# A four-layer graph network: how the running maxima of a window's 16 chunk ends are chained on VectorE

## The chip, the cores and the metric

The kernel runs on one core of one Trainium2 chip. The metric is the device time of one execution in microseconds (us), as the median of several executions. PE is TensorE, DVE is VectorE, ACT is ScalarE, POOL is GpSimd and SP is SyncE, which here only starts DMAs.

## The reference

Four graph layers run one after the other on 3125 nodes of 256 features and 50,000 edges; each is followed by a residual sum and a layer norm. Layers 1 and 2 are attention layers. For each edge a score per head is computed (4 heads in layer 1, 8 in layer 2), and then a softmax over all edges that end in the same node:

```python
m = jax.ops.segment_max(score, col_idx, num_segments=n)
ex = jnp.exp(score - m[col_idx])
denom = jax.ops.segment_sum(ex, col_idx, num_segments=n)
alpha = ex / denom[col_idx]
agg = jax.ops.segment_sum(alpha[..., None] * msg_edge, col_idx, num_segments=n)
```

The edges are sorted by their target node, so a node's edges are a run of neighbours in the order (a segment). The first two layers' inputs are gathered rows of tables, 128 edges at a time.

## The kernel before

**Chunks and windows.** The sorted edges are laid out in NCH = 416 chunks of 128 edges, one edge per partition. WIN = 16 chunks make a window, so each attention layer ("pass") has NW = 26 windows. `Attend` holds what both passes share, `Attend1` (4 heads, names a1, rows of 516 values) and `Attend2` (8 heads, a2, rows of 520 values) what differs. POOL gathers one row per edge into a ring of 36 slots by an indirect DMA per chunk (L2132), and it may refill a slot when PE has summed the chunk that lay in it.

**The work on a chunk.** In pass 1, PE fetches the queries of the chunk's targets with a one-hot matmul (L2480, three products for each chunk), DVE multiplies them with the gathered keys for two chunks at a time (L2494) and reduces four chunks' products at a time to scores (L2501). In pass 2 a score is only a sum of two gathered numbers (L2593, L2597). When the scores of a whole window are there, the window's chain gives the exponentials. Then ACT multiplies the values with them (L2531 in pass 1, L2624 in pass 2, where DVE does every other part, L2613), PE sums the chunk by target with a one-hot matrix (`total`, L2535 or L2629), and DVE adds the sum to the accumulator of the node tile (`add`, L2538 or L2635). `total(n)` waits until the sum of chunk n - 3 (pass 1) or n - 2 (pass 2) has been added, because its PSUM banks are used in turn. `add(n)` waits until `add(n - 1)` has ended. Before `add(n)` with n a multiple of 8, DVE's sequencer loads eight tile numbers into registers (`slots`).

**The loop.** Each engine runs a loop over w (the window whose chain is made) and i = 0..15. In step i of window w the engine also works on chunk n = 16 (w - 1) + i of the window before, and on scores of the window behind. So chain, sums and scores are woven together in the fixed order of each engine's own program. The tables `CHAIN`, `TURNS`, `SCORES` and `FETCHES` say at which i a part stands; for DVE an entry (i, False) stands ahead of `add(n - 2)` and (i, True) behind it.

**The chain of a window.** (1) PE turns the scores so that a row is one chunk and one head with its 128 edges in a line ("score", i = 5 in pass 1). (2) `run` and `most` are a forward and a backward scan over the 128 edges, with state = max(state + mask, value); a mask entry is 0 inside a segment and -1e30 where one ends. `most` is then the maximum of each segment within its chunk. (3) A segment can go on over several chunks. So the first and the last entry of each row are picked (`ends_in`) and a matmul (`ends`) brings them to one row per head: 16 values of the first edges and 16 of the last edges. Ten small DVE operations on [heads, 16] tiles then carry the maximum over the chunks, with the row vectors `seams` (0 where a chunk goes on with the segment that the chunk before it ended in), `whole` (0 where a chunk is one segment) and `through` (their sum): `carry` (scan), `onto`, `lead`, `past`, `tail`, two copies of one element, `last_in` (backward scan), `through`, `first`. They are at (8, False), (8, True), (9, False) and (9, True). (4) A matmul (`spread`, i = 10) brings the results `first_last` back to the rows; `picked`, `edge`, `most_1` and `most_2` put them into the row maxima. (5) PE turns `most_2` back ("back", L2383, i = 12 in pass 1 and 13 in pass 2), DVE makes `fall` (L2281, how much the maximum of the open node rose) and `below` (score minus maximum), and ACT makes the exponentials behind `keep_r` (L2335, i = 14).

**Order between engines** is by semaphores alone. Every step of the chain adds one to the semaphore `chain`; `after(name)` makes the sequencer wait until that step has ended:

```python
if at == here["lead"]:
    after("onto")
    step("lead", e.tensor_tensor(self.lead[:, :], self.onto[:, :], small[0:H, 0:WIN], ALU.max))
    after("lead")
    step("past", e.tensor_tensor(self.past[:, 0:WIN - 1], self.lead[:, 1:WIN], seams[:, 1:WIN], ALU.add))
```

`Segments.vector_ends` makes `seams`, `whole` and `through` once, in the stage ahead of pass 1.

Of the kernel before, what the change touches and what calls it, by code (L numbers as in the profile page):

```python
# [15 lines left out]
BF16 = mybir.dt.bfloat16  # L16
U16 = mybir.dt.uint16
ALU = mybir.AluOpType
# [1926 lines left out]
class Segments:  # L1945
# [3 lines left out]
    def __init__(self, b, ctx, slot_rows):  # L1949
        sb = lambda n, s, d=F32: b.sb(n, s, d, ctx)  # L1950
        self.seams, self.whole, self.through = (sb(n, [H2, NCH], BF16) for n in ("seams", "whole", "through"))
# [61 lines left out]
    def vector_ends(self, e):  # L2013

        kept, finish = self.kept, self.finish
        e.wait_ge(self.back, 16 * 3)
        e.memset(self.seams[:, 0:1], 0.0)
        e.tensor_tensor(self.seams[:, 1:NCH], self.first[:, 1:NCH], self.last[:, 0:NCH - 1], ALU.is_equal)
        e.tensor_tensor(self.whole[:, :], self.first[:, :], self.last[:, :], ALU.is_equal)
        e.tensor_copy(self.opens[:, :], self.local_f[:, 0:NCH:WIN]).then_inc(kept, 1)  # L2020
        e.wait_ge(kept, 4)
        finish(e, self.seams[:, :], self.seams[:, :])
        finish(e, self.whole[:, :], self.whole[:, :]).then_inc(kept, 1)
        e.wait_ge(kept, 5)
        e.tensor_tensor(self.through[:, :], self.seams[:, :], self.whole[:, :], ALU.add).then_inc(kept, 1)
        e.wait_ge(kept, 6)
# [16 lines left out]
class Attend:  # L2043


    def __init__(self, b, seg, own, name, heads, acc, table, word, stride, parts, x, lent=0):
# [10 lines left out]
        if x is not None:  # L2057
# [10 lines left out]
        self.ends_in, self.picked, self.edge = sb("ends_in", [R, 2, WIN]), sb("picked", [R, 2, WIN]), sb("edge", [R, 2])  # L2068
        self.carry = sb("carry", [H, 2, WIN + 1])
        self.onto, self.lead, self.past, self.tail = (sb(n, [H, WIN]) for n in ("onto", "lead", "past", "tail"))  # L2070
        self.last_in, self.first_last = sb("last_in", [H, WIN]), sb("first_last", [H, 2, WIN])
# [14 lines left out]
    STEPS = ("run", "most", "ends_in", "open", "carry", "onto", "lead", "past", "tail", "last_in", "through", "first",  # L2086
             "picked", "edge", "most_1", "most_2", "fall", "below")
# [73 lines left out]
    def constants_vector(self, e):  # L2161
# [4 lines left out]
        e.memset(self.carry[:, 0, 0:1], -BIG)  # L2166
# [25 lines left out]
    def vector(self, e):  # L2192
# [23 lines left out]
        def chain(w, i, late):  # L2216
# [7 lines left out]
            c = self.carry[:, w % 2, :]  # L2224
            both = self.first_last
            seams, whole, through = (t[0:H, w * WIN:(w + 1) * WIN] for t in (seg.seams, seg.whole, seg.through))
# [9 lines left out]
            if at == here["ends_in"]:  # L2236
                after("most")
                step("ends_in", e.tensor_tensor(self.ends_in[:, :, :], self.k1[:, :].unsqueeze(1).to_broadcast([R, 2, WIN]),
                                                self.most[:, 0:P:P - 1].unsqueeze(2).to_broadcast([R, 2, WIN]), ALU.mult))
# [4 lines left out]
            if at == here["carry"]:  # L2244
                e.wait_ge(self.ends_out, self.w0 + w + 1)
                step("carry", e.tensor_tensor_scan(c[:, 1:WIN + 1], through, small[0:H, WIN:2 * WIN], c[:, 0:1], ALU.add, ALU.max))
                after("carry")
                step("onto", e.tensor_tensor(self.onto[:, :], c[:, 0:WIN], seams, ALU.add))
            if at == here["lead"]:
                after("onto")  # L2250
                step("lead", e.tensor_tensor(self.lead[:, :], self.onto[:, :], small[0:H, 0:WIN], ALU.max))
                after("lead")
                step("past", e.tensor_tensor(self.past[:, 0:WIN - 1], self.lead[:, 1:WIN], seams[:, 1:WIN], ALU.add))
            if at == here["tail"]:
                after("past")
                step("tail", e.tensor_tensor(self.tail[:, 0:WIN - 1], self.past[:, 0:WIN - 1], c[:, 1:WIN], ALU.max))
                e.tensor_copy(both[:, 1, WIN - 1:WIN], c[:, WIN:WIN + 1])
                e.tensor_copy(self.carry[:, (w + 1) % 2, 0:1], c[:, WIN:WIN + 1])
                after("tail")
                step("last_in", e.tensor_tensor_scan(both[:, 1, WIN - 2::-1], through[:, :0:-1], self.tail[:, WIN - 2::-1],  # L2260
                                                     c[:, WIN:WIN + 1], ALU.add, ALU.max))
            if at == here["through"]:
                after("last_in")
                step("through", e.tensor_tensor(self.last_in[:, :], both[:, 1, :], whole, ALU.add))
                after("through")
                step("first", e.tensor_tensor(both[:, 0, :], self.last_in[:, :], self.lead[:, :], ALU.max))
            if at == here["picked"]:
                e.wait_ge(self.spread, self.w0 + w + 1)
                step("picked", e.tensor_tensor(self.picked[:, :, :], small[0:R, 64:64 + 2 * WIN].rearrange("r (a k) -> r a k", a=2),
                                               self.k1[:, :].unsqueeze(1).to_broadcast([R, 2, WIN]), ALU.mult))  # L2270
                after("picked")
                step("edge", e.tensor_reduce(self.edge[:, :], self.picked[:, :, :], AX_X, ALU.add))
# [1566 lines left out]
```

## Time and profile before

| | |
|---|---|
| median of 3 executions | 3441.07 us (3435.51 to 3443.51) |
| profiled execution, first to last instruction (span) | 3438.5 us |
| PE busy | 2897.5 us, 84% |
| DVE busy | 2544.3 us, 74% |
| POOL busy | 2183.2 us, 63% |
| ACT busy | 1935.0 us, 56% |
| mean granted PE clock | 0.884 |
| pass 1, `run` of window 0 to `run` of window 25 | 1384.2 to 1953.8 us |
| pass 2, the same | 2156.9 to 2703.0 us |

The page gives no time for the profiled execution besides its span, which lies between the lowest and the highest of the three times and 2.6 us under their median. The two passes take about 1130 us of it, a third. The busy shares are means over six stages that have little in common, so they say nothing of what a change in the passes is worth; the length of one window of a pass does.

### The profile page before, as it was taken

To read this page: it belongs to the slowest core of one execution; us is meant where nothing else is said; L and a number is where in the kernel's file an instruction comes from. 1 tells how busy PE (TensorE), PEld (TensorE's weight loads), DVE (VectorE), ACT (ScalarE), POOL (GpSimd) and SP (SyncE) were. 2 spreads that over 40 slices of the span, in tenths; PEclk is the share of its full clock that TensorE was granted. 3 is DMA by queue.
4 is the path that set the end of the run, shared out by engine and by line. 5 is a ranking of instruction groups with operands and counts; after the bars stand their busy time and mean duration, and the time that the engine had idled before them with its cause. 6 is when DMAs were issued, how large, how long until landed. Compare 5 with 4: busy or idle time off the path is not lost. (4 is left out here: it accounts for less than half of the span.)

```text
span 3438.5 us, 60509 instructions
## 1 busy us (share of the span) xinstructions
PE 2897.5 (84%) x15715; PEld 1839.2 (53%) x15715; DVE 2544.3 (74%) x6536; ACT 1935.0 (56%) x6284; POOL 2183.2 (63%) x2289
## 2 busy tenths in 40 slices
PE   5799889999988896788888866899999897788875
PEld 4666555555555553455555544677777653333332
DVE  8899789999977554888888843799999874444444
ACT  0478655555541452687788722688888753333333
POOL 1777677777756532766666355777777314777774
PEclk9999899999999998798899988899999996655665
DMA  5334388888851789777777555777777444333334
GB/s 179 100 104 130 121 256 261 260 265 264 261 138 34 242 324 351 243 229 220 218 209 212 128 186 184 224 227 227 228 228 226 117 199 162 104 103 103 103 104 103
DMA packets 260604, 651.44 MB, mean 189 GB/s; under 512 B 66781, under 2 KB 115626, under 8 KB 253498
## 3 DMA queue, kind: packets, MB, share of 16 engines
q0 software_dynamic: 141840, 474.50, 45.9%
q1 hardware_dynamic: 118442, 173.08, 15.5%
q8 instruction: 149, 2.44, 0.3%
q14 instruction: 173, 1.42, 0.1%
HBM read 505.42 MB, written 145.27 MB: 189 GB/s over the span
## 5 line engine op out<-in xcount | busy, mean ns | idle before, releaser
L2132 POOL DMA_INDIRECT a_rows<-table,met x568 | 560.3, 987 | 241.1 <-issue 137.8
L3729 PE MATMUL ps<-rows_in,hot_w 128*128 128x256 f32 x832 | 431.5, 630 | 114.2 <-ACT hot_w L3691 68.5
L1330 POOL DMA_INDIRECT rows_in<-table,met x416 | 413.1, 993 | 142.9 <-issue 80.3
L3679 POOL DMA_INDIRECT rows_in<-table,met x416 | 404.2, 972 | 144.3 <-issue 118.3
L3754 DVE TENSOR_TENSOR xs<-xs,ps 128x256 f32 x416 | 175.1, 421 | 302.7 <-PE ps L3729 298.1
L3729 PEld LDWEIGHTS ps<-rows_in,hot_w 128*128 128x128 f32 x832 | 192.6, 284 | 353.1 <-ACT hot_w L3691 199.2
L3691 ACT ACTIVATE hot_w<-hot,met 128x128 f32<-128x128 f32 x416 | 166.7, 402 | 372.1 <-PE ps L3729 353.9
L2629 PE MATMUL ps<-a_rows,a_hot 128*128 128x260 f32 x1136 | 316.4, 402 | 18.2 <-DVE acc L2635 12.7
L2132 POOL DMA_INDIRECT xs<-table,met x264 | 258.7, 980 | 107.3 <-issue 61.3
L833 POOL DMA_INDIRECT records<-rec,rows x241 | 260.5, 1081 | 87.6 <-issue 72.9
L2635 DVE TENSOR_TENSOR acc<-acc,ps 128x520 f32 x416 | 287.0, 690 | 34.6 <-PE ps L2629 13.6
L2624 ACT ACTIVATE a_rows<-a_rows 128x64 f32<-128x64 f32 x1136 | 281.2, 334 | 0.0
L2531 ACT ACTIVATE a_rows<-a_rows 128x64 f32<-128x64 f32 x1104 | 274.2, 335 | 0.0
L1362 ACT ACTIVATE z<-z 128x512 f32<-128x512 f32 x208 | 131.1, 631 | 243.8 <-DVE z L1491 243.8
L1440 PE MATMUL ps<-rows_in,hot_w 128*128 128x272 f32 x832 | 244.5, 417 | 3.7 <-ACT hot_w L1377 3.7
L1403 PE MATMUL ps<-by_dst,hot_t 128*128 x1248 | 212.0, 278 | 35.7 <-issue 32.0
L2629 PEld LDWEIGHTS ps<-a_rows,a_hot 128*128 128x128 f32 x1136 | 194.5, 191 | 68.4 <-issue 32.9
L2480 PE MATMUL ps<-q_parts,a_hot_t 128*128 x1248 | 208.9, 312 | 14.7 <-DVE a_prod L2494 8.2
L2535 PE MATMUL ps<-a_rows,a_hot 128*128 128x260 f32 x568 | 197.5, 441 | 26.2 <-DVE acc L2538 22.2
L1476 DVE TENSOR_TENSOR acc<-acc,ps 128x272 f32 x416 | 180.6, 434 | 47.4 <-DVE acc L1476 42.0
L2538 DVE TENSOR_TENSOR acc<-acc,ps 128x260 f32 x416 | 174.1, 419 | 50.0 <-issue 22.4
L620 ACT ACTIVATE film_room<-film_room,code_parts 128x128 bf16<-128x128 bf16 x648 | 191.7, 387 | 20.2 <-DVE film_room L716 20.2
(492 smaller groups left out, 6417.3 us busy)
## 6 DMA issues: line engine op xcount, KB each, us to landing
a_hot_t<-one_hots SPq DMA_DIRECT2D x104, 256.0 KB, 5.0
table<-stage SPq DMA_DIRECT2D x25, 1024.0 KB, 3.9
rows_in<-table,met POOLq DMA_INDIRECT x832, 3.8
one_hots<-hot_t SPq DMA_DIRECT2D x52, 256.0 KB
dst_row<-slot_rows SPq DMA_DIRECT2D x51, 256.0 KB, 5.0
by_dst<-dst_rows SPq DMA_DIRECT2D x25, 512.0 KB, 5.7
by_dst<-lo_rows SPq DMA_DIRECT2D x24, 512.0 KB, 4.4
a_rows<-table,met POOLq DMA_INDIRECT x568, 3.8
```

The source lines that it names most:

```text
L833: e.indirect_dma_start(b.meta, bass.IndirectOffsetOnAxis(ap=r.rows[:, c:c + 1], axis=0), r.rec[:, c, :], None).then_inc(s, 16)
L1330: e.indirect_dma_start(self.rows[:, n % self.RING, 0:2 * D], None, self.table, bass.IndirectOffsetOnAxis(ap=self.b.met[:, n, R_SRC:R_SRC + ...
L1403: e.matmul(out, self.hot_t[:, half, k, :], row[:, m * D:(m + 1) * D], start=(m == 0), stop=False)
L1440: e.matmul(b.ps[:, 4 + n % 4, 0:D + ET], self.hot_w[:, n % self.AHEAD, :], self.rows[:, n % self.RING, D:2 * D + ET], start=True, stop=Tru ...
L2132: e.indirect_dma_start(self.row(n, 0, self.width), None, self.table, bass.IndirectOffsetOnAxis(ap=b.met[:, n, self.word:self.word + 1], ax ...
L2480: last = e.matmul(out, hot_t, row[:, k * D:(k + 1) * D], start=(k == 0), stop=(k == 2))
L2531: last = e.mul(value, value, row[:, 2 * D + h:2 * D + h + 1])
L2624: last = e.mul(value, value, row[:, h:h + 1])
L2629: last = e.matmul(self.b.ps[:, 2 + 2 * (n % 2) + g, 0:GW2], hot, self.group(n, g), start=True, stop=True)
L2635: return e.tensor_tensor(both, both, self.b.ps[:, at:at + G2, 0:GW2], ALU.add)
L3679: e.indirect_dma_start(self.rows[:, n % self.RING, :], None, self.table, bass.IndirectOffsetOnAxis(ap=self.b.met[:, n, R_REL:R_REL + 1], a ...
L3729: e.matmul(b.ps[:, n % self.BANKS, 0:D], self.hot_w[:, n % GRP_H, :], self.rows[:, n % self.RING, :], start=True, stop=True).then_inc(self ...
```

## The change

The two ends of a chunk are put next to each other: one row of 32 entries per head holds first edge, last edge, first edge, last edge and so on, where there were two rows of 16. One mask row `links` with the same layout (the link into a chunk, then the link through it) takes the place of `seams`, `whole` and `through`; it has one more pair at its end, filled by a memset. A forward scan (`ahead`) over 32 entries and a backward scan (`both`) over the result give what the ten steps gave. The last entry of `ahead` is the carry into the next window, kept in two buffers in turn. `ahead` stands at (8, False) and `both` at (8, True); nothing of the chain is left at i = 9. PE's matmuls `ends`, `spread` and the others stay at their i, and `spread` waits for `both` where it waited for `first`. `ends_in` and `picked` have the same number of elements in another order, `edge` reduces along a stride of two. The core of the diff:

```diff
-        self.seams, self.whole, self.through = (sb(n, [H2, NCH], BF16) for n in ("seams", "whole", "through"))
+        self.links = sb("links", [H2, NCH + 1, 2], BF16)
...
-        e.memset(self.seams[:, 0:1], 0.0)
-        e.tensor_tensor(self.seams[:, 1:NCH], self.first[:, 1:NCH], self.last[:, 0:NCH - 1], ALU.is_equal)
-        e.tensor_tensor(self.whole[:, :], self.first[:, :], self.last[:, :], ALU.is_equal)
+        e.memset(self.links[:, 0, 0:1], 0.0)
+        e.memset(self.links[:, NCH, 0:2], 0.0)
+        e.tensor_tensor(self.links[:, 1:NCH, 0], self.first[:, 1:NCH], self.last[:, 0:NCH - 1], ALU.is_equal)
+        e.tensor_tensor(self.links[:, 0:NCH, 1], self.first[:, :], self.last[:, :], ALU.is_equal)
         e.tensor_copy(self.opens[:, :], self.local_f[:, 0:NCH:WIN]).then_inc(kept, 1)
         e.wait_ge(kept, 4)
-        finish(e, self.seams[:, :], self.seams[:, :])
-        finish(e, self.whole[:, :], self.whole[:, :]).then_inc(kept, 1)
+        finish(e, self.links[:, :, :], self.links[:, :, :]).then_inc(kept, 1)
         e.wait_ge(kept, 5)
-        e.tensor_tensor(self.through[:, :], self.seams[:, :], self.whole[:, :], ALU.add).then_inc(kept, 1)
-        e.wait_ge(kept, 6)
 
...
-        self.ends_in, self.picked, self.edge = sb("ends_in", [R, 2, WIN]), sb("picked", [R, 2, WIN]), sb("edge", [R, 2])
-        self.carry = sb("carry", [H, 2, WIN + 1])
-        self.onto, self.lead, self.past, self.tail = (sb(n, [H, WIN]) for n in ("onto", "lead", "past", "tail"))
-        self.last_in, self.first_last = sb("last_in", [H, WIN]), sb("first_last", [H, 2, WIN])
+        self.ends_in, self.picked, self.edge = sb("ends_in", [R, WIN, 2]), sb("picked", [R, WIN, 2]), sb("edge", [R, 2])
+        self.ahead, self.both = sb("ahead", [H, 2, 2 * WIN]), sb("both", [H, 2 * WIN])
...
-    STEPS = ("run", "most", "ends_in", "open", "carry", "onto", "lead", "past", "tail", "last_in", "through", "first",
-             "picked", "edge", "most_1", "most_2", "fall", "below")
+    STEPS = ("run", "most", "ends_in", "open", "ahead", "both", "picked", "edge", "most_1", "most_2", "fall", "below")
...
-        e.memset(self.carry[:, 0, 0:1], -BIG)
+        e.memset(self.ahead[:, 1, 2 * WIN - 1:2 * WIN], -BIG)
...
-            c = self.carry[:, w % 2, :]
-            both = self.first_last
-            seams, whole, through = (t[0:H, w * WIN:(w + 1) * WIN] for t in (seg.seams, seg.whole, seg.through))
+            ahead, before = self.ahead[:, w % 2, :], self.ahead[:, (w + 1) % 2, 2 * WIN - 1:2 * WIN]
+            links = seg.links[0:H, :, :].rearrange("h k a -> h (k a)")
+            at_0 = 2 * w * WIN
...
-                step("ends_in", e.tensor_tensor(self.ends_in[:, :, :], self.k1[:, :].unsqueeze(1).to_broadcast([R, 2, WIN]),
-                                                self.most[:, 0:P:P - 1].unsqueeze(2).to_broadcast([R, 2, WIN]), ALU.mult))
+                step("ends_in", e.tensor_tensor(self.ends_in[:, :, :], self.k1[:, :].unsqueeze(2).to_broadcast([R, WIN, 2]),
+                                                self.most[:, 0:P:P - 1].unsqueeze(1).to_broadcast([R, WIN, 2]), ALU.mult))
                 if w:
                     e.wait_ge(self.scale_out, self.w0 + w)
                 step("open", e.tensor_scalar(self.open_hot[:, :], b.iota[0:H, :], d0, None, ALU.is_equal))
-            if at == here["carry"]:
+            if at == here["ahead"]:
                 e.wait_ge(self.ends_out, self.w0 + w + 1)
-                step("carry", e.tensor_tensor_scan(c[:, 1:WIN + 1], through, small[0:H, WIN:2 * WIN], c[:, 0:1], ALU.add, ALU.max))
-                after("carry")
-                step("onto", e.tensor_tensor(self.onto[:, :], c[:, 0:WIN], seams, ALU.add))
-            if at == here["lead"]:
-                after("onto")
-                step("lead", e.tensor_tensor(self.lead[:, :], self.onto[:, :], small[0:H, 0:WIN], ALU.max))
-                after("lead")
-                step("past", e.tensor_tensor(self.past[:, 0:WIN - 1], self.lead[:, 1:WIN], seams[:, 1:WIN], ALU.add))
-            if at == here["tail"]:
-                after("past")
-                step("tail", e.tensor_tensor(self.tail[:, 0:WIN - 1], self.past[:, 0:WIN - 1], c[:, 1:WIN], ALU.max))
-                e.tensor_copy(both[:, 1, WIN - 1:WIN], c[:, WIN:WIN + 1])
-                e.tensor_copy(self.carry[:, (w + 1) % 2, 0:1], c[:, WIN:WIN + 1])
-                after("tail")
-                step("last_in", e.tensor_tensor_scan(both[:, 1, WIN - 2::-1], through[:, :0:-1], self.tail[:, WIN - 2::-1],
-                                                     c[:, WIN:WIN + 1], ALU.add, ALU.max))
-            if at == here["through"]:
-                after("last_in")
-                step("through", e.tensor_tensor(self.last_in[:, :], both[:, 1, :], whole, ALU.add))
-                after("through")
-                step("first", e.tensor_tensor(both[:, 0, :], self.last_in[:, :], self.lead[:, :], ALU.max))
+                step("ahead", e.tensor_tensor_scan(ahead, links[:, at_0:at_0 + 2 * WIN], small[0:H, 0:2 * WIN], before, ALU.add, ALU.max))
+            if at == here["both"]:
+                after("ahead")
+                step("both", e.tensor_tensor_scan(self.both[:, ::-1], links[:, at_0 + 1:at_0 + 2 * WIN + 1][:, ::-1], ahead[:, ::-1],
+                                                  -BIG, ALU.add, ALU.max))
             if at == here["picked"]:
                 e.wait_ge(self.spread, self.w0 + w + 1)
-                step("picked", e.tensor_tensor(self.picked[:, :, :], small[0:R, 64:64 + 2 * WIN].rearrange("r (a k) -> r a k", a=2),
-                                               self.k1[:, :].unsqueeze(1).to_broadcast([R, 2, WIN]), ALU.mult))
+                step("picked", e.tensor_tensor(self.picked[:, :, :], small[0:R, 64:64 + 2 * WIN].rearrange("r (k a) -> r k a", a=2),
+                                               self.k1[:, :].unsqueeze(2).to_broadcast([R, WIN, 2]), ALU.mult))
                 after("picked")
-                step("edge", e.tensor_reduce(self.edge[:, :], self.picked[:, :, :], AX_X, ALU.add))
+                step("edge", e.tensor_reduce(self.edge[:, :], self.picked[:, :, :].rearrange("r k a -> r a k"), AX_X, ALU.add))
...
-                step("fall", e.tensor_scalar(self.fall[:, :], both[:, 0, 0:1], c[:, 0:1], 0.0, ALU.subtract, ALU.max))
+                step("fall", e.tensor_scalar(self.fall[:, :], self.both[:, 0:1], before, 0.0, ALU.subtract, ALU.max))
...
-            flat = lambda t: t[:, :, :].rearrange("r a k -> r (a k)")
-                e.matmul(small[0:H, 0:2 * WIN], self.of_head[:, :], flat(self.ends_in), start=True, stop=True).then_inc(self.ends_out, 1)
+                e.matmul(small[0:H, 0:2 * WIN], self.of_head[:, :], self.ends_in[:, :, :].rearrange("r k a -> r (k a)"), start=True, stop=True).then_inc(self.ends_out, 1)
-                e.wait_ge(self.chain, self.chained(w, "first"))
-                e.matmul(small[0:R, 64:64 + 2 * WIN], self.to_rows[:, :], flat(self.first_last), start=True, stop=True).then_inc(self.spread, 1)
+                e.wait_ge(self.chain, self.chained(w, "both"))
+                e.matmul(small[0:R, 64:64 + 2 * WIN], self.to_rows[:, :], self.both[:, :], start=True, stop=True).then_inc(self.spread, 1)
...
-    CHAIN = {"run": (5, True), "most": (6, False), "ends_in": (6, True), "carry": (8, False), "lead": (8, True), "tail": (9, False),
-             "through": (9, True), "picked": (10, True), "most_1": (11, False), "fall": (11, True), "below": (12, False)}
+    CHAIN = {"run": (5, True), "most": (6, False), "ends_in": (6, True), "ahead": (8, False), "both": (8, True), "picked": (10, True), "most_1": (11, False), "fall": (11, True), "below": (12, False)}
```

The same `CHAIN` edit stands in `Attend2`. STEPS has 12 names for 18, so `chain` counts to other values. The wait behind `vector_ends` in the stage ahead of pass 1 is for `kept` 5 where it was 6. Nothing else of the kernel is touched.

## Rows read from the trace of the kernel before

**Rows 1.** Busy time of each engine in the steady part of pass 1 and of pass 2 (us; PE, PEld, DVE, ACT, POOL, each with its instructions, then granted PE clock, DMA share, GB/s).

```profile
1405.00:1954.00 549.00, 457.84 (x2541) 308.15 (x2540) 476.15 (x1202) 442.35 (x1745) 359.80 (x378) 0.89 0.74 215
2199.00:2681.00 482.00, 459.26 (x3042) 343.13 (x3041) 438.67 (x1075) 409.75 (x1604) 359.38 (x354) 1.00 0.78 227
```

**Rows 2.** The scan `run` in each pass: count, ns min/median/max, first and last start.

```profile
L2232 DVE TENSOR_TENSOR_SCAN a_run<-a_mask,ps x25: 403/405/405, 1405.3 to 1953.8; 64x128 f32<-64x128 bf16 x25
L2232 DVE TENSOR_TENSOR_SCAN a_run<-a_mask,ps x23: 409/411/414, 2199.6 to 2680.3; 128x128 f32<-128x128 bf16 x23
```

**Rows 3.** Waits from 1400 to 2040 us: us in total, times, longest.

```profile
ACT a_keep_r L2335 <- DVE a_fall L2281: 63.1, 24, 3.1
...
PE ps L2383 <- DVE a_most L2277: 52.5, 25, 2.4
...
PE ps L2535 <- DVE acc L2538: 31.9, 85, 1.2
```

**Rows 4.** DVE timeline of one window of pass 1: start, us, and in brackets idle before.

```profile
1704.16 0.23 DVE L2246 TENSOR_TENSOR_SCAN a_carry<-through,a_carry,ps 4x16 f32<-4x16 bf16 x1
...
1704.61 0.42 DVE L2538 TENSOR_TENSOR acc<-acc,ps 128x260 f32 x1
...
1705.61 0.23 DVE L2260 TENSOR_TENSOR_SCAN a_first_last<-through,a_carry,a_tail 4x15 f32<-4x15 bf16 x1
1705.78 0.42 DVE L2538 TENSOR_TENSOR acc<-acc,ps 128x260 f32 x1
...
1706.31 0.16 DVE L2266 TENSOR_TENSOR a_first_last<-a_last_in,a_lead 4x16 f32<-4x16 f32 x1
1707.37 0.42 DVE L2538 TENSOR_TENSOR acc<-acc,ps 128x260 f32 x1 [0.90 <-issue]
```

**Rows 5.** PE timeline of the same window, around its wait for the chain.

```profile
1707.94 0.68 PE L2535 MATMUL ps<-a_rows,a_hot 128*128 128x260 f32 x2 [0.48 <-DVE acc L2538]
...
1710.76 0.37 PE L2383 MATMUL ps<-ident,a_most 64*128 64x64 f32 x1 [2.15 <-DVE a_most L2277]
```

**Rows 6.** Groups of DVE instructions by shape, both passes: busy us, mean ns | idle before.

```profile
L2235 DVE TENSOR_TENSOR_SCAN a_most<-a_mask,a_run 64x128 f32<-64x128 bf16 x26 | 10.8, 414 | 0.9
...
L2246 DVE TENSOR_TENSOR_SCAN a_carry<-through,a_carry,ps 4x16 f32<-4x16 bf16 x26 | 5.9, 226 | 0.0
```

**Rows 7.** Columns of rows 1: behind a stall, and two whole windows of pass 1.

```profile
1711.50:1717.50 6.00, 6.00 (x27) 4.15 (x27) 4.91 (x9) 5.74 (x23) 2.80 (x3) 0.53 0.70 225
...
1611.20:1633.30 22.10, 18.47 (x108) 12.53 (x106) 19.64 (x51) 17.97 (x72) 15.50 (x17) 0.92 0.78 229
...
1701.80:1725.20 23.40, 19.82 (x108) 13.26 (x106) 19.97 (x51) 18.35 (x73) 14.38 (x16) 0.85 0.66 197
```

**Rows 8.** DVE timeline, the one wait for PE of over 0.25 us in the window from 1611.2.

```profile
1626.52 0.42 DVE L2538 TENSOR_TENSOR acc<-acc,ps 128x260 f32 x1 [0.67 <-PE ps L2535]
```

**Rows 9.** PE timeline at shorter stalls of another stage.

```profile
407.06 0.21 PE L673 MATMUL ps<-prod,above 25*25 25x1 f32 x2 [0.59 <-DVE prod L772]
407.96 0.96 PE L675 MATMUL ps<-reached,ones 25*128 25x416 f32 x2 [0.70 <-DVE reached L776]
...
1063.29 1.97 PE L1673 MATMUL ps<-up,h_t 128*128 128x256 f32 x8 [1.14 <-DVE y L1749]
```

**Rows 10.** Columns of rows 1: the granted clock at the stalls of rows 9.

```profile
409.00:413.00 4.00, 4.00 (x15) 1.82 (x14) 0.54 (x1) 0.00 (x0) 0.96 (x1) 0.60 0.72 180
1062.00:1066.00 4.00, 2.86 (x15) 2.43 (x14) 3.03 (x8) 0.89 (x3) 3.41 (x5) 1.00 0.21 68
```

**Rows 11.** POOL timeline in pass 1, one of the gathers that follow one another.

```profile
1630.41 0.95 POOL L2132 DMA_INDIRECT a_rows<-table,met  x1 [0.30 <-issue]
```

**Rows 12.** Waits from 2160 to 2720 us (pass 2): us in total, times, longest.

```profile
PE ps L2629 <- DVE acc L2635: 19.1, 90, 0.5
```

**Rows 13.** PE timeline in pass 2 beside the chain's small steps (DVE makes them from 2421.76 to 2424.56).

```profile
2423.31 1.11 PE L2629 MATMUL ps<-a_rows,a_hot 128*128 128x260 f32 x4
...
2424.64 1.12 PE L2629 MATMUL ps<-a_rows,a_hot 128*128 128x260 f32 x4
```

More of the change, by code:

```diff
@@ L2554 @@
     TURNS, HOT_AT, OTHER_AT = {"score": 3, "ends": 7, "spread": 10, "back": 13}, 2, 8
-    CHAIN = {"run": (4, True), "most": (5, True), "ends_in": (6, True), "carry": (8, False), "lead": (8, True), "tail": (9, False),
-             "through": (9, True), "picked": (11, True), "most_1": (12, True), "fall": (13, False), "below": (14, False)}
+    CHAIN = {"run": (4, True), "most": (5, True), "ends_in": (6, True), "ahead": (8, False), "both": (8, True), "picked": (11, True), "most_1": (12, True), "fall": (13, False), "below": (14, False)}
     def __init__(self, b, seg, own, acc, table, parts, x):
@@ L2765, in sync @@
         self.seg.sync(e)
-        e.wait_ge(self.seg.kept, 6)
+        e.wait_ge(self.seg.kept, 5)
         for t in range(NS - self.QS, NS):
```

## The prediction

> **What bounds the kernel now.** I read the page's slices first: the two passes are stages in which PE, DVE, ACT and POOL are all busy, so the table by stage comes next [rows 1]. DVE is busy for 87% of pass 1 and 91% of pass 2, PE for 83% and 95%; the granted clock is 0.89 in pass 1 and 1.00 in pass 2. The unit to reason in is the window. From the first and last `run` scan a window takes (1953.8 - 1405.3) / 24 = 22.85 us in pass 1 and (2680.3 - 2199.6) / 22 = 21.85 us in pass 2 [rows 2].
>
> In pass 1 the waits say who is late [rows 3]: PE waits for `most_2` 25 times, 52.5 us together, and ACT for `fall` 24 times, 63.1 us. That is 2.1 and 2.6 us in each window, and both ends of the wait are the chain on DVE. The DVE timeline shows why: from `carry` to the `add` of chunk 8, at 1704.16 to 1707.37, DVE goes from one small step to the next with no gap of its own but the 0.90 us of `slots` [rows 4]. PE stops 2.15 us for the result [rows 5]. So DVE sets the time from i = 0 to i = 12, and a microsecond taken from it there comes out of the window, as long as PE still waits at "back".
>
> Behind each such stall PE runs at the lower clock: from 1711.5 to 1717.5 the mean granted clock is 0.53, where 0.50 is 1.2 of 2.4 GHz, and PE is busy all six microseconds [rows 7]. There PE sets the time, and DVE waits for it; even in one of the short windows it waits 0.67 us in one piece [rows 8]. The two whole windows show what it costs. At a mean clock of 0.92 the low stretch is 2 x 0.08 x 22.1 = 3.5 us long, at 0.85 it is 2 x 0.15 x 23.4 = 7.0 us, and the windows last 22.1 and 23.4 us: 1.3 / 3.5 = 0.37 us for each us of low clock. At the pass's mean of 0.89 that is 5.0 us of it and 1.9 us of time in each window, an estimate by a straight line.
>
> **The change, part by part.** *What it takes away.* Ten operations between `carry` and the `add` of chunk 8. Start to start this stretch is 1707.37 - 1704.16 = 3.21 us, with two adds (chunks 6 and 7) in it.
>
> *What it puts there.* Two scans of 32 entries. No row has this width. Scans of 128 take 0.414 us and scans of 16 take 0.226 us [rows 6], so 32 lies between them; on the line between them it is 0.226 + 16 x 0.188 / 112 = 0.253 us, which I take, since 32 is nearer to 16. The upper end would add 2 x 0.16 = 0.32 us to each window. Start to start counts, not the record: `last_in` (0.23) is followed by an independent `add` after 0.17 [rows 4], so 0.06 of a record lies under the next. New stretch: `ahead` 0.19, `add` of chunk 6 0.34 (0.42 less some 0.08), `both` 0.19, then `add` of chunk 7 and the `add` of chunk 8 behind its eight register loads. From `first` to that `add` it takes 1.06 now [rows 4], and the loads can start when chunk 7's `add` has been handed over, so again 1.06. Sum 0.19 + 0.34 + 0.19 + 1.06 = 1.78 us, which saves 3.21 - 1.78 = 1.43 us. If the loads hid nothing and both scans cost the upper end, 0.7 us would be left; if the loads hid under `both` too, 1.6.
>
> The waits of `both` on `ahead` cost nothing: the `add` of chunk 6 lies between them. If it did not, it would be some 0.07 us. `spread` stays at i = 10, and `both` is ready well ahead of it.
>
> *Where the stall goes.* The `add` of chunk 8 comes 1.43 earlier too, and PE's sum of chunk 11 waited 0.48 us for it [rows 5]. With that and its short wait for `first` gone PE reaches "back" about 0.7 us earlier and `most_2` comes 1.43 earlier: the stall shrinks from 2.15 to about 1.45 us. It is still there, so DVE is still what sets the time and the whole 1.43 counts: x 25 windows (the first starts behind other waits) = 35.8 us.
>
> *Equal work in another order.* `ends_in`, `picked`, `edge`: the same elements, at strides; `fall`, the masks and the PE matmuls: unchanged in size. `vector_ends` loses one tensor addition, once, before pass 1. All these count as nothing; DVE has no wait on their layout that a row could show, and if each of the three cost 0.05 us more on DVE, it would be 0.15 x 25 = 4 us, which is inside the range.
>
> *The clock.* Does PE keep 2.4 GHz through a stall of 1.45 us? The rows on both sides are near: 1.14 us of waiting kept it at 1.00, while 0.59 and 0.70 us of waiting close together were followed by a mean of 0.60 [rows 9, 10]. So I expect most windows to drop as before and let one in four keep the clock. If a window keeps it, the 1.9 us come back only as far as POOL allows: a gather takes 0.95 + 0.30 = 1.25 us [rows 11], sixteen 20.0, and some 20.2 with the slower ones. From 22.85 - 1.43 = 21.42 that leaves 1.2 us. One in four: 0.3 x 25 = 7.5 us; none 0; all 30.
>
> The Trainium skill, "TensorE: Matmul & The Clock Gate", Part 1, says that the throttled clock is the default and recent activity lifts it. The falls behind stalls in pass 1 agree (clock 0.53 behind a 2.15 us wait); by that rule alone a shorter stall can only help, and the time would tend to the all-windows case below.
>
> The skill's "DVE: opcode table, instruction layouts, handler registers and perf-mode slots", section 6, speaks against wide scans: the built-in scan runs at half throughput. The two scan rows differ by 0.188 us over 112 entries, 1.7 ns an entry. At the clock in "VectorE: DVE Perf Modes" (0.96 GHz), half throughput would be 2.1 ns, an estimate, and the 32 added entries would cost 0.07 us a window instead of 0.05: no matter here.
>
> *Pass 2.* PE is busy 95% [rows 1] and runs its sums back to back beside the chain's small steps: 1.11 us from 2423.31, then other matmuls, then the next sum at 2424.64 with no wait named [rows 13]. Its waits for DVE adds sum to 19.1 us in 90 pieces [rows 12], 0.7 us a window, mostly away from these steps. So the removed work lies under PE. Bounds 0 and 19 us; I take 3.
>
> *Sum.* 35.8 + 7.5 + 3 = 46 us off the span of 3438.5, to 3392; the median of the runs is 2.6 us above that span, so 3394.6, which I give as 3394.
>
> **The rivals.** *A, my forecast:* pass 1 gives the chain's 1.43 us, a minority of windows keeps the clock: 3385 to 3410.
>
> *B, the clock stays up in nearly all windows of pass 1.* For it: the shorter stall, and the 1.14 us that was survived. Against: the pair of 0.59 and 0.70 that was not. Then a window meets POOL's 20.2: (22.85 - 20.2) x 25 = 66, and 3 in pass 2: 3372; with half of the windows 3387.
>
> *C, part of the gain is taken by another engine in pass 1.* POOL is already at its 1.25 us cadence over long runs, and ACT, which waits 2.6 us now, would have 1.2 left. If half of the 1.43 goes, and the clock gives nothing: 18 + 1 off, 3422. For it: ACT, PE and POOL are all above 65% in pass 1. Against: each has over 1.43 us of waiting in a window.
>
> *D, nothing measurable:* the window is set by PE and the chain only fills DVE's wait for it. It would be 3434 to 3448. Against it stand the 52.5 us in which PE waits. That two scans cost what ten steps did is excluded by the 0.414 us row.
>
> *E, slower: the lower clock spreads.* Windows end at another point against the clock's changes, and the low stretch behind the stall could get longer. It decides when it grows by more than 1.43 / 0.37 = 3.9 us, from 5.0 to 8.9 us. If it grew to 12 us in each window: 7 x 0.37 - 1.43 = 1.16 us, x 25 = 29 slower, 3470. Against: 7.0 us is the longest in the rows of whole windows.
>
> **How the numbers follow.** A 0.60, B 0.17, C 0.16, D 0.04, E 0.03. No more than about 0.2% of the time (7 us) can be told from no change here. Faster is A, B and C: 0.93; same is D: 0.04; slower is E: 0.03. The predicted time is A's 3394. The range leaves out D, E, the upper part of C and nothing of B: 3372 to 3420.
>
> **What the profile after would show.** `ahead` and `both` at 0.24 to 0.27 us each. 8 x 52 = 416 fewer DVE instructions in the passes. Carry-to-chunk-8 stretch 1.8 us, not 3.2. PE's wait for `most_2` about 1.4 us a window and ACT's for `fall` about 1.2. Windows of 21.1 us on the mean in pass 1 and 21.7 in pass 2. The granted clock of pass 1 near 0.90; at 0.97 or more it is B. It is wrong if pass 1's window stays above 22.3 us: then look at who waits for POOL or ACT; or if pass 2 gives more than 10 us: then its small waits were the chain's after all.

## The result and the profile after

The changed kernel takes 3375.7 us as the median of 4 runs (3367.1 to 3377.2), beside 3438.3 us for the kernel before: the ratio is 0.9814, 95% interval 0.9802 to 0.9826. The profiled execution took 3374.4 us with a span of 3372.5 us. That is 63 us less where 46 us of saving was forecast; it lies in the range, 18 us below the point and outside the 3385 to 3410 us of forecast A itself.

First where the 66 us between the two spans lie. Below are the scan `run` of the kernel after, in pass 1, in an undisturbed part of it, and in pass 2 (each its own answer; count, ns, first and last start).

```profile
L2227 DVE TENSOR_TENSOR_SCAN a_run<-a_mask,ps x25: 404/404/405, 1398.4 to 1894.1; 64x128 f32<-64x128 bf16 x25
...
L2227 DVE TENSOR_TENSOR_SCAN a_run<-a_mask,ps x19: 404/404/405, 1440.9 to 1808.7; 64x128 f32<-64x128 bf16 x19
...
L2227 DVE TENSOR_TENSOR_SCAN a_run<-a_mask,ps x24: 410/412/418, 2119.8 to 2613.8; 128x128 f32<-128x128 bf16 x24
```

A window of pass 1 takes (1894.1 - 1398.4) / 24 = 20.65 us, where it took 22.85; one of pass 2 takes 494.0 / 23 = 21.48 us, where it took 21.85 [rows 2]. From `run` of window 0 to `run` of window 25, pass 1 went from 569.6 to 516.5 us (its `run` of window 0 is at 1377.6 now) and pass 2 from 546.1 to 537.9 us: 53.1 and 8.2 us less. Pass 1 also began 6.6 us earlier. That is no work of the scans: in three other kernels below, which have the same work ahead of it but for the mask rows, it began at 1380.2, 1380.7 and 1383.0 us. Between and behind the passes 1.9 us were lost again.

The DVE timeline of the kernel after, one window of pass 1, answers to rows 4.

```profile
1607.06 0.26 DVE L2241 TENSOR_TENSOR_SCAN a_ahead<-links,a_ahead,ps 4x32 f32<-4x32 bf16 x1
1607.25 0.39 DVE L2515 TENSOR_TENSOR acc<-acc,ps 128x260 f32 x1
1607.56 0.20 DVE L2244 TENSOR_TENSOR_SCAN a_both<-links,a_ahead 4x32 f32<-4x32 bf16 x1
1607.85 0.43 DVE L2515 TENSOR_TENSOR acc<-acc,ps 128x260 f32 x1
1608.92 0.43 DVE L2515 TENSOR_TENSOR acc<-acc,ps 128x260 f32 x1 [0.65 <-PE ps L2512]
```

From `ahead` to the `add` of chunk 8 it is 1.86 us (3.21 before, 1.78 forecast). The bracket names PE, but PE's sum of chunk 8 had ended at 1607.51; the `add` of chunk 8 starts 1.07 us after that of chunk 7, and that is the eight register loads again, as in rows 4. A wait goes to the last event the trace knows of, and the loads leave no event of their own.

PE's place for the turn back, and the granted clock behind it (columns of rows 1):

```profile
1612.31 0.27 PE L2361 MATMUL ps<-ident,a_most 64*128 64x64 f32 x1 [1.90 <-DVE a_most L2256]
```

```profile
1612.30:1620.30 8.00, 7.75 (x55) 5.83 (x56) 7.51 (x15) 7.45 (x31) 6.13 (x7) 1.00 0.85 273
1816.30:1819.30 3.00, 2.94 (x13) 2.07 (x14) 2.38 (x7) 2.55 (x11) 2.39 (x3) 0.50 0.83 225
```

The stall is 1.90 us in nearly every window, not the 1.45 that was forecast, and the clock stays at 1.00 behind 19 of the 24 stalls from 1406.0 to 1880.1, one of 2.15 us among them. Before, it fell at each stall from 1414.2 to 1939.3, as in the windows of rows 7. In the second line, behind a wait of 1.91 us at 1816.29, it is 0.50. The steady part of pass 1 (columns of rows 1) has a mean granted clock of 0.98, where it had 0.89:

```profile
1398.00:1894.00 496.00, 417.95 (x2540) 284.58 (x2540) 449.58 (x1009) 444.67 (x1749) 360.06 (x379) 0.98 0.79 238
```

The prediction had said that 0.97 or more would mean rival B, and that is what the trace shows. Here, with the chain at its new length, the 19 windows at full clock from 1419.7 us on took 20.5 us on the mean, and the four whole windows from 1808.7 us on, each with a low stretch, 21.3 us.

Nine of the twelve kernels below were timed in three sets in which every kernel, the kernel before among them, took 13 to 14% longer (medians of 3861 to 3968 us), so each kernel is compared with the kernel before of its own set.

### The profile page after: what moved, and what is told of

The parts are those of the page before. It is cut to its first block and busy times, and to the rows that moved or that the text cites. A ratio compares the mean times of both kernels' runs of the same rounds, so it can differ in the third digit from the quotient of the medians.

```text
span 3372.5 us, 60092 instructions
## 1 busy us (share of the span) xinstructions
PE 2869.2 (85%) x15715; PEld 1820.4 (54%) x15715; DVE 2490.2 (74%) x6119; ACT 1936.3 (57%) x6284; POOL 2164.4 (64%) x2289
## 5 line engine op out<-in xcount | busy, mean ns | idle before, releaser
L2127 POOL DMA_INDIRECT a_rows<-table,met x568 | 548.9, 966 | 213.7 <-issue 135.3
L3705 PE MATMUL ps<-rows_in,hot_w 128*128 128x256 f32 x832 | 450.3, 655 | 96.0 <-ACT hot_w L3667 53.3
L3705 PEld LDWEIGHTS ps<-rows_in,hot_w 128*128 128x128 f32 x832 | 200.1, 295 | 346.2 <-ACT hot_w L3667 185.7
L2605 PE MATMUL ps<-a_rows,a_hot 128*128 128x260 f32 x1136 | 316.6, 403 | 18.1 <-DVE acc L2611 12.6
L2457 PE MATMUL ps<-q_parts,a_hot_t 128*128 x1248 | 189.0, 290 | 18.8 <-DVE a_prod L2471 10.0
L2512 PE MATMUL ps<-a_rows,a_hot 128*128 128x260 f32 x568 | 183.8, 418 | 18.1 <-DVE acc L2515 9.8
```

Of the source, the lines that this page charges most:

```text
L2127: e.indirect_dma_start(self.row(n, 0, self.width), None, self.table, bass.IndirectOffsetOnAxis(ap=b.met[:, n, self.word:self.word + 1], ax ...
L2605: last = e.matmul(self.b.ps[:, 2 + 2 * (n % 2) + g, 0:GW2], hot, self.group(n, g), start=True, stop=True)
L3705: e.matmul(b.ps[:, n % self.BANKS, 0:D], self.hot_w[:, n % GRP_H, :], self.rows[:, n % self.RING, :], start=True, stop=True).then_inc(self ...
```

## The experiments

### The clock by itself

The kernel before, with PE kept busy in its stall:

```diff
             if i == self.TURNS["back"]:
+                for _ in range(13):        # pass 1 only
+                    e.matmul(b.ps[:, self.BACK, 256:512], b.ident_b[:, :], self.parts[:, 0, 0:256], start=True, stop=True)
                 e.wait_ge(self.chain, self.chained(w, "most_2"))
```

> The kernel before with 13 matmuls of no use in PE's wait for the chain in pass 1, once more, because the first chip ran every kernel at some 3920 us with long gaps in all engines, in which nothing of the change can be seen. On a chip where the kernel before takes about 3440 us: if the lower clock costs time, the granted clock of pass 1 goes to 0.97 or more, its windows from 22.85 to 21.6 to 22.0 us and the time to 3408 to 3418 us; if the lower clock only fills time in which PE would wait, 3435 us or more.

Measured: 3410.8 us beside 3435.9 us, ratio 0.9923 (0.9906 to 0.9939). Its busy time in pass 1 (columns of rows 1):

```profile
1401.00:1923.00 522.00, 450.86 (x2851) 307.67 (x2851) 472.89 (x1201) 444.17 (x1745) 358.75 (x378) 1.00 0.76 226
```

And its `run` scans there:

```profile
L2232 DVE TENSOR_TENSOR_SCAN a_run<-a_mask,ps x25: 404/404/405, 1401.3 to 1923.1; 64x128 f32<-64x128 bf16 x25
```

At a granted clock of 1.00 and with all ten steps in place, the window is 521.8 / 24 = 21.74 us. So the lower clock cost 22.85 - 21.74 = 1.1 us a window, 25 to 28 us in all, and the ten steps cost the rest: against the undisturbed windows of the kernel after, (1808.7 - 1440.9) / 18 = 20.43 us, it is 1.31 us a window. The rule of the Trainium skill's "TensorE: Matmul & The Clock Gate", Part 1 (throttled by default, released by activity), is borne out: PE had more to do, its granted clock went from 0.89 to 1.00, and the kernel got faster. Its pass 2, with the old code, stayed at (2652.5 - 2147.5) / 23 = 21.96 us.

### The length of the chain, and when the clock falls

The changed kernel with a DVE operation of no use in pass 1:

```diff
+            if at == (8, True):            # pass 1 only, behind "both"
+                one = self.k1_t[0:1, 0, 0:1].unsqueeze(2).to_broadcast([1, 1, 1230])
+                e.tensor_tensor(self.pad[:, :, :], one, one, ALU.max)
```

> The changed kernel with one DVE operation of no use (1230 elements, some 1.4 us) behind the second scan in pass 1, on another chip than the slow ones. If only the length of DVE's work at this place counts, pass 1's windows go from 20.4 to 21.8 us at full clock, or to 22.8 us with the lower clock behind the stalls: 3411 or 3428 us where the kernel before takes 3438. If the ten steps cost by their number, under 3400 us.

Measured: 3402.8 us beside 3437.3, ratio 0.9898 (0.9882 to 0.9915), which is neither number. The DVE timeline of one window:

```profile
1601.61 0.26 DVE L2243 TENSOR_TENSOR_SCAN a_ahead<-links,a_ahead,ps 4x32 f32<-4x32 bf16 x1
...
1602.25 1.40 DVE L2249 TENSOR_TENSOR a_pad<-a_k_t 1x1230 f32<-1x1230 f32 x1
1603.58 0.41 DVE L2520 TENSOR_TENSOR acc<-acc,ps 128x260 f32 x1
1604.19 0.43 DVE L2520 TENSOR_TENSOR acc<-acc,ps 128x260 f32 x1 [0.21 <-DVE acc L2520]
```

The operation holds DVE for 1.33 us, but the stretch grew only from 1.86 to 2.58 us, by 0.72: chunk 8's `add` now follows after 0.61 us in place of 1.07, since the register loads run under the long operation. So what counts is not the record of an operation but what it adds to the stretch. Between the kernels before and after the loads make no difference: they hold up chunk 8's `add` by 1.06 us behind `first` and by 1.07 us behind chunk 7's `add`. The added 0.72 us comes out in the window in full: 20.43 + 0.72 = 21.15 us, and the four windows of this run that lie at full clock from end to end took 21.1 to 21.5 us. The other twenty took 22.1 us on the mean.

PE's rows at two turns back of this run, and the clock behind them:

```profile
1586.52 0.27 PE L2365 MATMUL ps<-ident,a_most 64*128 64x64 f32 x1 [2.21 <-DVE a_most L2260]
...
1541.77 0.36 PE L2365 MATMUL ps<-ident,a_most 64*128 64x64 f32 x1 [2.21 <-DVE a_most L2260]
```

```profile
1586.50:1594.50 8.00, 7.70 (x55) 5.83 (x56) 7.51 (x15) 7.30 (x29) 6.17 (x7) 1.00 0.96 287
1541.80:1544.30 2.50, 2.44 (x11) 1.70 (x12) 2.22 (x7) 1.98 (x8) 1.89 (x3) 0.50 0.80 193
```

The same wait of 2.21 us, longer than the 2.15 us behind which the clock fell in most windows before, left it at 1.00 four times out of 24 and was followed by 0.50 twenty times (the 24 waits are 2.19 to 2.36 us). The window with the clock up at 1586.5 lasts 21.1 us, the one at 1541.8 lasts 22.7 us. So the length of the stall does not decide alone; something of when it falls must. Over the traces the length has its weight all the same. The clock fell at all 24 stalls of 2.15 to 2.37 us in the kernel before and at 20 of 24 in this run; at 5 of 24 in the kernel after and at 6 of 24 in the run with the loads moved, below (nearly all 1.90 us, one of 2.15 in each); and at none of 24 with the 13 matmuls in them, which leave 0.73 to 0.95 us. The place of a fall is not tied to the stall: in the kernel after the clock went down 0.3 us before PE went on at 1816.29, in the next three windows 1.45, 1.08 and 0.74 us after it went on, when PE was busy again. Why it came out well so often in the kernel after is argued, not shown: its windows are all nearly the same length (20.3 to 20.9 us from 1440.9 to 1808.7), and the clock fell behind the first stall, stayed up behind the next 19 and fell behind the last four, as if a stall's place in time decided and nearly equal windows kept that place from one to the next. The page of the Trainium skill named above says in Part 1 that activity is judged over periods that run by themselves and do not start anew with the kernel; the places of the falls agree with that (0.3 us ahead of PE's going on to 1.45 us behind it), and no run here shows the periods themselves. The run meant for this question ("late", below) cannot be read.

### What pass 2 gave, and PE's register loads

PE's timeline in pass 2, kernel before and then kernel after: the six fetch matmuls at i = 12, ahead of which PE's sequencer loads eight registers.

```profile
2428.36 0.79 PE L2583 MATMUL ps<-a_parts,a_hot_t 128*128 x6
```

```profile
2388.22 0.37 PE L2559 MATMUL ps<-a_parts,a_hot_t 128*128 x6
```

0.42 us less in this window, and the window is 0.37 us shorter. Over 22 windows of each trace the group at i = 12 took 0.69 us before and 0.34 after (medians), and the one at i = 8, which loads registers too, 0.68 and 0.69. The groups of six at the six other places take 0.29 to 0.30, so the rest of a merged row is a pause in it. An explanation that no run tests: before the group PE's sequencer stands at a sum that waits for DVE's `add` two chunks back; a late `add` lets it go late, and the loads then lie open for longer. The ten steps would have made DVE's adds late there. The waits for adds themselves did not change: 19.1 us before [rows 12], 19.0 us after:

```profile
PE ps L2605 <- DVE acc L2611: 19.0, 93, 0.5
```

To test whether the pause is the loads, they were moved in the changed kernel:

```diff
-                if m % 8 == 0:
+                if m == 0:
                     self.at = self.slots(e, regs, m)
                 self.fetch(e, m, ...)
+                if m % 8 == 7 and m + 1 < NCH:
+                    self.at = self.slots(e, regs, m + 1)
```

> The changed kernel with one addition: PE loads the next eight tile numbers right behind the last fetch that used the old ones, in place of right before the next fetch, in both passes; no matmul of no use. If PE's open register loads are what is left of the term that pass 2 gave (the group of six fetch matmuls at i = 8 took 0.65 us in the changed kernel, 0.30 in the run before this one), pass 2's windows fall from 21.45 to 21.1 us and the time by 8 to 9 us, to 3367. If DVE's adds take the time over, nothing comes of it: 3374 to 3378. On a chip on which the kernel before takes 3900 us, only the length of the group can be read.

Measured: 3376.2 us beside 3438.1, ratio 0.9828 (0.9800 to 0.9856): the kernel after, not better. PE's timeline in its pass 2:

```profile
2385.27 0.29 PE L2561 MATMUL ps<-a_parts,a_hot_t 128*128 x6
...
2395.11 1.11 PE L2607 MATMUL ps<-xs,a_hot 128*128 128x260 f32 x4 [0.52 <-issue]
```

The group at i = 8 is down to 0.29 us as expected, and the loads now stand open ahead of a sum, 0.52 us. The window is (2614.5 - 2124.5) / 23 = 21.30 us, 0.18 less, not 0.35: 5 us, and they are within what pass 1 and the runs vary by. All 176 groups of 22 windows take 0.29 to 0.30 us now, so the pause in them was the loads, and a pause with no named wait stands ahead of sums instead: the loads are on PE's path wherever they stand. That the scans shortened the pause, and not the place at which pass 1 ended, is borne out by two more traces. With the two scans and the operation of no use in pass 1, pass 2 stayed at (2644.7 - 2151.5) / 23 = 21.44 us and the group at i = 12 at 0.34; with the ten steps and PE kept busy in pass 1 it was 21.96 us and 0.66. How the ten steps lengthened it stays argued.

### The runs in the three slower sets

Nine runs in three sets. The mixtures keep both chains in one kernel, each pass with its own:

```diff
+        chain = chain_old if self.OLD else chain_new      # OLD: True in one pass, False in the other
```

> The two scans stand in pass 1 alone; pass 2 keeps its ten steps (both sets of mask rows are made, once, about 2 us of DVE work ahead of pass 1). If pass 1 gives its part by itself and pass 2 gave the 0.4 us a window that its windows fell by (21.85 to 21.45 us), this run is about 10 us above the changed kernel: 3386 us. If pass 2's windows were shorter only because of where pass 1 ended, it is at 3376 to 3379 us.

> The two scans stand in pass 2 alone. If pass 2 gives 10 us by itself: 3428 us, pass 2 windows of 21.4 to 21.5 us and pass 1 windows of 22.8 us with the lower clock behind each stall. If the step of my prediction was right that the removed work lies under PE there: 3435 us or more, windows of 21.7 us or more.

> The two scans in pass 1 alone, once more, on another chip than the first time. If pass 2's shorter windows (21.45 for 21.85 us) are the scans' own doing, this run lacks them: 3386 us where the changed kernel takes 3376. If they come from outside of pass 2, 3376 to 3379 us, and pass 2's windows stay at 21.5 us with the ten steps in them.

Two kernels are those of above, the kernel before with PE busy in its stall and the kernel after with 1230 elements in the chain:

> The kernel before, with 13 matmuls of no use (128x128 bf16 weights, 256 columns, into a free part of the bank that PE turns into) at the place where PE waits for the chain in pass 1, so that PE is busy for some 1.4 of the 2.15 us. It prices the clock alone, with the ten steps in place. If the lower clock costs time: the granted clock of pass 1 goes from 0.89 to 0.97 or more, the windows from 22.85 to 21.6 to 22.0 us, 3408 to 3418 us in all. If DVE sets the whole window and the lower clock only fills time in which PE would wait, 3435 us or more.

> The changed kernel, with one DVE operation of no use behind the second scan in pass 1, on one partition with 1230 elements, some 1.4 us: the time that the ten steps took more than the two scans. If only the length of DVE's work at this place counts, pass 1 falls back to windows of 22.6 to 22.9 us with the lower clock behind the stalls, 3424 to 3430 us in all (pass 2 keeps its gain). If the ten steps cost by their number (waits between steps, the register loads that could not start), the window stays under 21.9 us and the time under 3405 us.

> The changed kernel, with one DVE operation of no use behind the second scan in pass 1, on one partition with 1230 elements, some 1.4 us: what the ten steps took more than the two scans. If only the length of DVE's work counts, pass 1's windows go from 20.4 to 21.8 us at full clock, or to 22.8 us with the lower clock behind the stalls, and the time to 3411 or to 3428 us (pass 2 keeps its gain). If the ten steps cost by their number, the time stays under 3400 us.

"Late" has a smaller operation of no use where PE does not wait for DVE, "lighter" leaves out half of the features in two of the four score reductions of pass 1, and the last one has the loads moved as above and 12 matmuls in the stall:

```diff
+            if at == (13, True):           # late: pass 1 only, 640 elements
+                e.tensor_tensor(self.pad[:, :, :], one, one, ALU.max)
```

```diff
+        part = DK // 2 if j in (1, 5) else DK
-                        ...rearrange("p a c (h f) -> p (a c h) f", h=H1), AX_X, ALU.add
+                        ...rearrange("p a c (h f) -> p (a c h) f", h=H1)[:, :, 0:part], AX_X, ALU.add
```

> The changed kernel, with one DVE operation of no use of 640 elements (some 0.75 us) at i = 13 in pass 1, behind the chain, so that the window gets longer and PE's stall at the turn back stays 1.9 us. If the length of the stall decides on the clock, the clock stays up as in the changed kernel, windows are 21.1 us and the time is 3393 us. If it is where the stalls fall in time that decides, the lower clock comes back in many windows: 21.6 to 22 us, 3405 to 3415 us.

> The changed kernel with two of a window's four score reductions in pass 1 (pairs 1 and 5) over the first half of each head's features only: the scores there are wrong, and DVE has 1.1 us less to do in each window. If POOL's cadence (16 gathers of 1.25 us, 20.0 us) is the next bound, the windows stay at 20.2 us or more and the time at 3372 us or more. If DVE is still the bound, the windows fall to 19.3 us and the time to 3350 us.

> The changed kernel with two additions. (1) PE loads the next eight tile numbers right behind the last fetch that used the old ones, in place of right before the next fetch, in both passes. (2) 12 matmuls of no use in PE's remaining 1.9 us stall in pass 1. If pass 2's windows fell from 21.85 to 21.45 us because PE's register loads no longer stood open (the group of six fetch matmuls took 0.37 us for 0.79), then the loads that still do (0.65 us for 0.30 at i = 8) give another 0.3 us a window: 21.1 us, 8 us in all; if PE's queue hides them anyway, 0. If the lower clock still costs in five windows of pass 1, the filler gives 1.1 us in each of them, 5 us; POOL's 20.0 us forbids more. Together 3362 us, where the changed kernel takes 3376; 3376 if neither is right.

| run | us | before | ratio, 95% interval |
|---|---|---|---|
| scans in pass 1 only | 3911.7 | 3927.1 | 0.9968 (0.9955 to 0.9981) |
| scans in pass 2 only | 3923.3 | 3927.1 | 0.9995 (0.9980 to 1.0011) |
| before, PE busy in the stall | 3925.9 | 3927.1 | 1.0005 (0.9984 to 1.0025) |
| after, 1230 elements in the chain | 3921.0 | 3927.1 | 0.9981 (0.9967 to 0.9995) |
| scans in pass 1 only, again | 3861.3 | 3880.6 | 0.9955 (0.9933 to 0.9977) |
| after, 1230 elements, again | 3873.6 | 3880.6 | 0.9989 (0.9969 to 1.0009) |
| after, 640 elements late | 3863.8 | 3880.6 | 0.9952 (0.9935 to 0.9970) |
| after, lighter | 3867.2 | 3880.6 | 0.9963 (0.9944 to 0.9982) |
| after, loads moved, PE busy | 3968.4 | 3930.0 | 1.0108 (1.0045 to 1.0171) |

They show what the scans in pass 1 are worth when something else holds the engines up: 0.3 to 0.5%. In the first of them the `run` scans give a window of (2246.5 - 1644.7) / 24 = 25.08 us, and these are two of its waits from 1700 to 2200 us, 20 windows:

```profile
L2246 DVE TENSOR_TENSOR_SCAN a_run<-a_mask,ps x25: 405/405/414, 1644.7 to 2246.5; 64x128 f32<-64x128 bf16 x25
```

```profile
ACT a_hot L2391 <- remote: 52.0, 27, 3.5
...
PE ps L2454 <- DVE a_most L2275: 22.7, 10, 4.4
```

ACT waits up to 3.5 us for an event that this trace lacks. PE still waits at the turn back, 22.7 us in 10 windows for `most_2` and 17.2 us in 8 others, put down there to steps ahead of it, up to 4.4 us where it was 2.4 at most before. POOL pauses up to 2.7 us before a gather while it waits for nothing that the trace shows; in pass 1 of the kernel before that was 0.3 us at most. A single `run` is as long as ever (0.405 us). What holds the engines up was not found. The expectations of these runs were made for windows of 20 to 23 us and can't be judged by them. So "lighter" does not say whether DVE or POOL bounds pass 1 of the kernel after (20.43 us against POOL's 16 x 1.25 = 20.0). The four windows of the run with 1230 elements speak for DVE: they grew by all that DVE had more to do, 0.72 us. The split by pass from a kernel with one pass changed stays open; the split above is from windows of the traces.

## Why the prediction was right

The number lies in the range; forecast A does not describe what happened. A had a minority of windows at full clock and 3385 to 3410 us; the kernel took 3375.7 us, with the clock up behind 19 of 24 stalls and at 0.98 over the pass, which is rival B (3372 us, chance 0.17). The range held because it had been drawn to take in B. The chain's part came as it was worked out, the clock's part did not.

- **DVE sets pass 1 from i = 0 to i = 12:** right. The chain's stretch shrank by 1.35 us (forecast 1.43) and windows at full clock by 1.31: about 33 us, where 35.8 were forecast. The 0.08 us that the stretch missed by lie behind `both`, where the `add` of chunk 7 started after 0.29 us and not after 0.19.
- **Two scans of 32 entries, 0.253 us each:** nearly right in sum, 0.26 and 0.205 us, 0.47 for 0.51. The register loads behind chunk 7's `add` took 1.07, as put in.
- **The stall shrinks to 1.45 us:** wrong by 0.45. PE reached "back" 1.9 us ahead of `most_2`, because its sum of chunk 11 moved forward by 1.1 us where the chain's stretch shrank by 1.35: from the start of `carry` to the end of that sum it was 4.46 us, from `ahead` 3.35. I had moved PE by 0.7 us only. It did no harm, since PE waits for DVE either way.
- **The clock, one window in four, 7.5 us:** this is the term that was mis-sized. Its price was nearly right: 1.1 us a window by the filled stall, where 1.2 was put in (the straight line through two windows gave 1.9, too much, and POOL's floor cut it to 1.2). Its count was wrong: 19 of 24 stalls kept the clock, not one in four. 53.1 us less the chain's 33 leaves 20 us. The step that failed is the one that read the count off the stall's length, from two other stages' rows [rows 9, 10]: stalls of 1.90 and even 2.21 us kept the clock at times. It was luck besides that the miss went the good way, since the stall was 0.45 us longer than the one from which the count had been taken.
- **Pass 2, 3 us:** 8 us. What came back was a pause inside a fetch group of merged matmuls (0.69 to 0.34 us), which no wait row names. I had read its waits for adds as the only cost that DVE could put on PE.
- **C and E:** no other engine took the gain (PE waits 1.90 us and POOL's window work is 20.0 us of 20.43), and the low stretches got rarer.
- The sum, 35.8 + 7.5 + 3 = 46, against 33 + 20 + 8 = 61, and 6.6 - 1.9 = 4.7 us by which the two executions differ outside the passes: together the 66 us between the spans. Between the medians it is 63.

## What to carry to other kernels

Where an engine sets the time, small dependent steps on it cost about what their records add up to: the ten steps' records in the window of rows 4 are 1.74 us and the two scans' 0.47, 1.27 less, and the window at full clock got 1.31 us shorter. Where another engine sets the time, as in pass 2, they can still cost (0.37 us a window here). Where PE stops for a result at the same place in every round, look at the granted clock behind it: a few matmuls of no use in the stall gave 0.8% here with the chain as it was, and they are the quick test for what the clock costs. A merged row that is longer than its like (0.79 for 0.29 us) is a pause to be explained, though no wait is listed.

## What was not expected of the hardware

- A stall of the same length (2.21 us) is followed by the lower clock in 20 windows and not in four others of one execution.
- The backward scan over 32 entries, all in SBUF and with a constant to begin with, takes 0.205 us, less than the backward scan over 15 entries that began with a value read from a tile (0.227 us) [rows 4 show it as 0.23]. The forward one, which reads PSUM and begins with such a value, takes 0.26.
